# Mixture-of-experts routing on one Trainium2 core: gate products of every second block of nodes on VectorE instead of TensorE

## The reference

```python
# xf: LayerNorm(x), 12500 x 256; 8 experts; the two best of each node are used
logits = xf @ gate_w + gate_b                      # 256 -> 8
probs = softmax(logits)
top2_vals, top2_idx = top_k(probs, 2)
cw = zeros((N, 8)).at[arange(N)[:, None], top2_idx].add(top2_vals)
# for each expert e
out += cw[:, e, None] * (gelu(xf @ W1[e] + b1[e]) @ W2[e] + b2[e])
# result: x + out
```

## Time and profile before

| | |
|---|---|
| median of 3 runs | 3413.88 us (3394.66 to 3414.95) |
| the profiled execution, whole | 3405.85 us |
| its span | 3403.8 us |
| granted TensorE clock, mean over the span | 0.912 of full speed |
| last stage, from the barrier | about 2376 to 3404 us |
| 105 expert slots, 210 adds to `out` on POOL | 332.5 us busy, 1583 ns each |

### The profile page before, as it was taken

One profiled execution on the slowest core, in us unless ns is written; L12 is line 12 of the kernel. 1 busy time (PEld: TensorE's weight loads), 2 busy tenths in 40 slices (PEclk: granted clock), 3 DMA queues, 4 the chain that ended last, 5 costly groups with the idle time before them and its releaser, 6 DMA issues.

```text
span 3403.8 us, 42546 instructions
## 1 busy us (share of the span) xinstructions
PE 2728.9 (80%) x11623; PEld 2100.2 (62%) x11623; DVE 2024.4 (59%) x5319; ACT 1570.9 (46%) x3411; POOL 2264.1 (67%) x2216
## 2 busy tenths in 40 slices
PE   6817767788888888888888878765279999899997
PEld 5706555566665665656665656543158778778886
DVE  7715556766666766766776666677635646544221
ACT  3405543445455455445455445533145555444442
POOL 0077777777777777777777777772647677666444
PEclk9959988899999999998999999887589999999998
DMA  7797766665665665665665665564756666656553
GB/s 237 245 285 217 201 182 164 166 175 159 171 182 155 173 175 160 170 180 161 172 176 163 166 184 157 153 179 100 272 141 165 145 158 165 144 127 138 101 90 48
DMA packets 403513, 570.77 MB, mean 168 GB/s; under 512 B 73177, under 2 KB 320239, under 8 KB 403098
## 3 DMA queue, kind: packets, MB, share of 16 engines
q0 software_dynamic: 125472, 300.85, 35.2%
q1 hardware_dynamic: 200569, 178.04, 17.9%
q10 hardware_dynamic: 77161, 88.52, 9.7%
HBM read 399.19 MB, written 183.46 MB: 171 GB/s over the span
## 4 chain that ended last, share of the span: by engine, by line
PE 57%; DMA 13%; POOL 9%; ACT 8%; issue 7%; DVE 5%; ACTq 1%; SPq 0%; POOLq 0%; DVEq 0%
PE bank L1196 21%; DMA rows<-table,srcix 10%; PE bank L2077 7%; PE bank L2090 7%; PE bank L1007 6%; POOL rows L1132 5%; PE bank L996 4%; PE bank L969 2%; DMA out<-x_y,x_dest 2%; POOL sorted_d L1619 2%; PE bank L784 2%; PE bank L554 1%; PE bank L555 1%; ACT L1232 1%; PE bank L1178 1%
## 5 line engine op out<-in xcount | busy, mean ns | idle before, releaser
L1132 POOL DMA_INDIRECT rows<-table,srcix x1664 | 1609.6, 967 | 506.9 <-issue 358.9
L1196 PE MATMUL bank<-rows,onehot 128*128 128x272 f32 x3328 | 942.7, 430 | 56.0 <-ACT fout L1246 54.3
L1246 ACT ACTIVATE fout<-bank 128x272 f32<-128x272 f32 x1664 | 639.6, 397 | 558.5 <-PE bank L1196 520.3
L1196 PEld LDWEIGHTS bank<-rows,onehot 128*128 128x128 f32 x3328 | 671.7, 210 | 248.5 <-ACT fout L1246 82.0
L1333 DVE TENSOR_TENSOR rows<-rows,bank 128x1024 f32<-128x1024 f32 x416 | 484.2, 1214 | 210.5 <-ACT rows L1237 210.2
L2162 POOL DMA_INDIRECT out<-x_y,x_dest x210 | 332.5, 1583 | 302.8 <-DMA out<-x_y,x_dest 172.0
L2077 PE MATMUL bank<-x_int,x_w1c 128*128 128x256 f32 x1680 | 394.2, 389 | 18.1 <-issue 10.9
L2090 PE MATMUL bank<-e_w,x_ht 128*128 x1680 | 383.7, 382 | 2.3 <-issue 2.3
L2077 PEld LDWEIGHTS bank<-x_int,x_w1c 128*128 128x128 f32 x1680 | 327.1, 196 | 70.0 <-issue 23.7
L2115 ACT ACTIVATE x_ht<-bank,x_b1c 128x256 f32<-128x256 f32 x420 | 174.2, 470 | 370.4 <-PE bank L2077 370.2
L2090 PEld LDWEIGHTS bank<-e_w,x_ht 128*128 128x128 f32 x1680 | 312.7, 191 | 46.3 <-issue 7.6
(11 more groups left out here) (355 smaller groups left out, 3346.9 us busy)
## 6 DMA issues: line engine op xcount, KB each, us to landing
frag<-fout ACTq DMA_DIRECT2D x104, 544.0 KB
x_in<-sorted_d SPq DMA_DIRECT2D x105, 260.0 KB, 3.4
rows<-table,srcix POOLq DMA_INDIRECT x1664
x_b2c<-in_L_ffn_b SPq DMA_DIRECT2D x105, 128.0 KB, 3.7
frag<-in_x ACTq DMA_DIRECT2D x1, 13416.0 KB
table<-hr SPq DMA_DIRECT2D x24, 544.0 KB, 3.6
xs<-in_x SPq DMA_DIRECT2D x24, 512.0 KB, 6.3
xnt_d<-xt SPq DMA_DIRECT2D x24, 512.0 KB, 5.0
```

Source lines behind the costliest of these rows:

```text
L1132: p.indirect_dma_start(out=B.rows[b][:, j, :], out_offset=None, in_=B.table[:, :], in_offset=bass.IndirectOffsetOnAxis(ap=B.srcix[:, col:c ...
L1196: pe.matmul(B.banks[2 + c % 3][:, 0:ROW], B.onehot[k % 2][:, j, :], B.rows[k % NR][:, j, :], start=True, stop=True).then_inc(S.sum, 1)
L1246: a.activation(B.fout[k % 2][:, j, :], B.banks[2 + c % 3][:, 0:ROW], ACT.Copy).then_inc(S.ev, 1)
```

## The change

In rounds 2 to 11 the gate products of the second super no longer go through PE. DVE multiplies each tile's normalized rows (128x256 of `e_hn`) with one expert's gate weights, spread over all partitions in the new `e_gw_all`, and the instruction (`scalar_tensor_tensor` with `accum_out`) also sums the products over the row into one number of `e_lgd`: 8 experts times 4 tiles, 32 instructions a round. `e_gw_all` is laid out [P, D, EXPERTS], so one expert's weights lie 8 words apart. The products themselves go to the scratch tile `e_gw_x`. Each instruction waits for the one before it. `gates` puts them down in 8 groups of 4, three steps apart (`GATES_GAP`), from step `GATES_AT` after the statistics on. Each group waits for its tile's `e_hn`.

PE's turns, gate matmuls and small turns, and ACT's copies, are made for `by_tensor(r)` alone: both supers in rounds 0 and 1, the first super from round 2 on. The bias addition becomes two, one from `e_lgd` and one from PE's bank. `e_hnt` shrinks to one super and `e_lgt` goes (its rows go over the used columns of the turned ones); rounds 0 and 1 use the expert buffers `x_ht`. `e_gw_all` is loaded by one DMA of SP, 1 MB over all partitions, behind the expert weights in round 0.

```diff
+GATES_AT, GATES_GAP = NORM + 4 - MOMENTS - MOMENT_STEPS, 3
+def by_tensor(r):
+    return ROUNDS[r] if r < FIRST_ROUNDS else ROUNDS[r][:1]
 ...
# Bufs
-        self.e_hn, self.e_hnt, self.e_st = several("e_hn", NH, [P, W, SENT]), A("e_hnt", [P, KD, W * P], F32), several("e_st", 2, [P, W, 16])
-        self.lgt = A("e_lgt", [EXPERTS, W * P], F32)
+        self.e_hn, self.e_hnt, self.e_st = several("e_hn", NH, [P, W, SENT]), A("e_hnt", [P, KD, ST * P], F32), several("e_st", 2, [P, W, 16])
+        self.gw_all, self.gw_x = A("e_gw_all", [P, D, EXPERTS], F32), A("e_gw_x", [P, D], F32)
+        self.lgd = A("e_lgd", [P, ST, EXPERTS], F32)
 ...
# route_sync, round 0, behind the loads of W1 and W2
+            sp.dma_start(B.gw_all[:, :, :].rearrange("p d e -> p (d e)"),
+                         B.a["L0_ffn_gate_w"].rearrange("d e -> (d e)").partition_broadcast(P)).then_inc(S.e_wd, 16)
 ...
# route_tensor (route_scalar's copies likewise)
-        for q, k in enumerate(ROUNDS[r]):
+        for q, k in enumerate(mine):          # mine = by_tensor(r)
 ...
-        for i in range(n):
+        for i in range(sum(SUPERS[k][1] for k in mine)):
 ...
# route_vector
+    def gates(r):
+        v.wait_ge(S.e_wd, 16)
+        for k in ROUNDS[r][1:]:
+            s, m = SUPERS[k]
+            for i in range(m):
+                for half in range(2):
+                    v.wait_ge(S.e_hn, s + i + 1)
+                    for e in range(half * EXPERTS // 2, (half + 1) * EXPERTS // 2):
+                        v.wait_ge(vec.sem, vec.n)
+                        vec(v.scalar_tensor_tensor(out=B.gw_x[:, :], in0=B.e_hn[r % NH][:, s - R_FIRST[r] + i, 0:D], scalar=1.0,
+                                                   in1=B.gw_all[:, :, e], op0=ALU.mult, op1=ALU.mult, accum_out=B.lgd[:, i, e:e + 1]))
+                    yield from idle(GATES_GAP)
 ...
+            if len(by_tensor(r)) < len(ROUNDS[r]):
+                own = sum(SUPERS[k][1] for k in ROUNDS[r][1:])
+                yield from idle(GATES_AT)
+                yield from gates(r)
+                waits -= GATES_AT + 2 * own * GATES_GAP
 ...
-        v.tensor_tensor(L, bk[3][:, GATES * EXPERTS:(GATES + n) * EXPERTS].rearrange("p (t e) -> p t e", t=n), over_tiles(B.gb[:, :]), ALU.add).then_inc(S.e_got, 1)
+        if of_pe < n:
+            v.wait_ge(vec.sem, vec.n)
+            vec(v.tensor_tensor(B.lg[:, of_pe:n, :], B.lgd[:, 0:n - of_pe, :], bias(n - of_pe), ALU.add))
+        v.tensor_tensor(B.lg[:, 0:of_pe, :], bk[3][:, GATES * EXPERTS:(GATES + of_pe) * EXPERTS].rearrange("p (t e) -> p t e", t=of_pe),
+                        bias(of_pe), ALU.add).then_inc(S.e_got, 1)
```

More of the change, by code:

```diff
@@ L158, in __init__ @@
             "mg_alpha_spread", "mg_alpha_copied", "mg_run_done", "mg_run_turned", "mg_part_ready", "mg_summed"))
+        self.e_wd = new("e_gate_spread_in")
         self.e_w, self.e_x, self.e_x1 = new("e_gate_in"), several("e_x_in", NF), several("e_x1_out", NF)
@@ L1560, with supers_to, turned @@
 GATES = 2 * P // EXPERTS
+GATES_AT, GATES_GAP = NORM + 4 - MOMENTS - MOMENT_STEPS, 3
 def placed(n):
     return BOTH + LAG + 1 + n + 6
+def by_tensor(r):
+    return ROUNDS[r] if r < FIRST_ROUNDS else ROUNDS[r][:1]
+def supers_to(r):
+    return sum(len(by_tensor(q)) for q in range(r))
 def turns_to(r):
-    return 3 * sum(len(q) for q in ROUNDS[:r])
+    return 3 * supers_to(r)
 def gates_to(r):
-    return sum(len(q) + 1 for q in ROUNDS[:r])
+    return supers_to(r) + r
+def turned(B, r, kk):
+    return B.ht[kk][:, :, :].rearrange("p k n -> p (k n)") if r < FIRST_ROUNDS else B.e_hnt[:, kk, :]
 def at_once(r):
@@ L1690, in steps @@
     def steps(r):
-        n = R_TILES[r]
+        n, mine = R_TILES[r], by_tensor(r)
         yield from idle(TURN)
-        for q, k in enumerate(ROUNDS[r]):
+        for q, k in enumerate(mine):
             s, m = SUPERS[k]
@@ L1702, in steps @@
             yield from idle(TURN_GAP)
-        yield from idle(GATE - TURN - TURN_GAP * len(ROUNDS[r]))
+        yield from idle(GATE - TURN - TURN_GAP * len(mine))
         pe.wait_ge(S.e_w, 32)
-        pe.wait_ge(S.e_t, turns_to(r) + 2 * len(ROUNDS[r]))
-        for i, k in enumerate(ROUNDS[r]):
+        pe.wait_ge(S.e_t, turns_to(r) + 2 * len(mine))
+        for i, k in enumerate(mine):
             s, m = SUPERS[k]
@@ L1709, in steps @@
             for kk in range(KD):
-                t = pe.matmul(bk[i][0:EXPERTS, 0:m * P], B.gw[:, kk, :], B.e_hnt[:, kk, o * P:(o + m) * P], start=(kk == 0), stop=(kk == KD - 1))
+                t = pe.matmul(bk[i][0:EXPERTS, 0:m * P], B.gw[:, kk, :], turned(B, r, kk)[:, o * P:(o + m) * P], start=(kk == 0), stop=(kk == KD - 1))
             t.then_inc(S.e_gate, 1)
@@ L1716, in steps @@
         pe.wait_ge(S.e_carry, r)
-        for i in range(n):
-            t = pe.transpose(bk[3][:, (GATES + i) * EXPERTS:(GATES + i + 1) * EXPERTS], B.lgt[:, i * P:(i + 1) * P],
+        for i in range(sum(SUPERS[k][1] for k in mine)):
+            t = pe.transpose(bk[3][:, (GATES + i) * EXPERTS:(GATES + i + 1) * EXPERTS], turned(B, r, 0)[0:EXPERTS, i * P:(i + 1) * P],
                              B.ident[0:EXPERTS, 0:EXPERTS])
@@ L1736, in steps @@
     def steps(r):
-        x, hn, st = B.e_x[r % NF], B.e_hn[r % NH], B.e_st[r % 2]
+        x, hn, st, theirs = B.e_x[r % NF], B.e_hn[r % NH], B.e_st[r % 2], by_tensor(r)
         yield from idle(NORM)
@@ L1758, in steps @@
         a.wait_ge(S.e_gate, gates_to(r))
-        for i, k in enumerate(ROUNDS[r]):
+        for i, k in enumerate(theirs):
             s, m = SUPERS[k]
@@ L1762, in steps @@
             for kk in range(KD):
-                a.wait_ge(S.e_tp, 2 * (2 * r + i) + kk + 1)
-                a.activation(B.e_hnt[:, kk, o * P:(o + m) * P], bk_columns(B, kk, m), ACT.Copy).then_inc(S.e_t, 1)
+                a.wait_ge(S.e_tp, 2 * (supers_to(r) + i) + kk + 1)
+                a.activation(turned(B, r, kk)[:, o * P:(o + m) * P], bk_columns(B, kk, m), ACT.Copy).then_inc(S.e_t, 1)
             yield from idle(TURN_GAP)
-        yield from idle(GATE + 1 - TURN - TURN_GAP * len(ROUNDS[r]))
-        for i, k in enumerate(ROUNDS[r]):
+        yield from idle(GATE + 1 - TURN - TURN_GAP * len(theirs))
+        for i, k in enumerate(theirs):
             s, m = SUPERS[k]
@@ L1770, in steps @@
             a.wait_ge(S.e_gate, gates_to(r) + i + 1)
-            a.activation(B.lgt[:, o * P:(o + m) * P], B.banks[i][0:EXPERTS, 0:m * P], ACT.Copy).then_inc(S.e_t, 1)
+            a.activation(turned(B, r, 0)[0:EXPERTS, o * P:(o + m) * P], B.banks[i][0:EXPERTS, 0:m * P], ACT.Copy).then_inc(S.e_t, 1)
         yield from idle(FRONT - GATE - 1)
@@ L1846, in steps @@
         v.wait_ge(S.e_w, 32)
-        v.tensor_tensor(L, bk[3][:, GATES * EXPERTS:(GATES + n) * EXPERTS].rearrange("p (t e) -> p t e", t=n), over_tiles(B.gb[:, :]), ALU.add).then_inc(S.e_got, 1)
+        of_pe = sum(SUPERS[k][1] for k in by_tensor(r))
+        bias = lambda m: B.gb[:, :].unsqueeze(1).to_broadcast([P, m, EXPERTS])
+        if of_pe < n:
[3 more added lines that the diff above has]
+                        bias(of_pe), ALU.add).then_inc(S.e_got, 1)
         yield
         v.wait_ge(S.e_got, r + 1)
+        v.wait_ge(vec.sem, vec.n)
         vec(v.tensor_reduce(s1[:, 0:n, 0], L, AX, ALU.max))
```

## The result

| | before | changed |
|---|---|---|
| median of 8 runs | 3412.13 us (3394.66 to 3414.95) | 3431.84 us (3426.83 to 3440.28) |
| ratio to before | | 1.0066, 95% interval 1.0052 to 1.0080 |
| profiled execution, whole | 3405.85 us | 3440.28 us |
| last stage begins (POOL's first memset) | 2375.8 us | 2380.3 us |

The changed kernel is 19.7 us (0.66%) slower. The two profiled executions stand 34 us apart because that of before is 6 us under its median and that of the changed kernel is the slowest of its eight. Their spans, 3403.8 and 3439.0 us, stand 35.2 apart. 4.5 us of that were already there when the last stage began, in code that is the same in both, so the stage itself shows 30.7. What follows adds up these 30.7 us of one pair of executions, not the 19.7 us between the medians.

The account below looks back on a forecast made before the run. POOL's own chain was taken to bound the last stage. +17 us at the start and +30 over eight rounds made 47, less about 8 at the end: net +39 on 3405.85, so 3445 us, range 3400 to 3480.

Parts of the forecast that it names:

- rival 1: Gate stride is free, DVE's round hidden; POOL's stretch, 15 us, and a few us at tile 4 remain: 3420; chance 0.27.
- The bound: Last stage, from tile 3 on: POOL's chain of issues and landings sets the pace; time taken from PE does not shorten it.
- What DVE gets: Rounds 2 to 11: 32 strided products a round, 0.66 us plus 0.08 for the sum; 0.77 each, 24.6 a round.
- The length of a round: Eight full rounds: DVE's list and waits take 64.8 us or more against 62.6; +3.7 a round, 30 us together.
- a sign that the prediction named against itself: The forecast is wrong if DVE keeps 10 us or more of idle time a round.
- The second price: POOL issues beginning within two-input gates are stretched, 0.25 us each, 2 to 3 us a round; not added.
- the sign against the queue: POOL's lag above 15 us through rounds 5 to 11 while the total grows: then the stretch is the price.
- The start: Rounds 2 and 3: gates delay the first tiles, +7 and +10 us, +17 in all.
- The end: After the last product: POOL is less behind, so the last 21.9 us shrink by about 8.
- Rival 2: PE was the bound, so its 31 us saving comes through and DVE hides the gates: 3375; chance 0.06.
- Rival 3: Sum needs a second pass, 35 us a round, or POOL and DVE hold each other whole instructions: 3535; chance 0.07.

Follow-up runs that it names:

- the first set: Four variants of the changed kernel (control, no gates, one-input gates, PE not relieved), timed against the kernel before, which took 3411.6 us: ratios 1.0063, 0.9986, 1.0028, 1.0065.
- the kernel nearest to before in the second set: Kernel before, its product by the node's weight made by two one-SBUF-input instructions: 3895.1 us, ratio 1.0034.
- the second set: Gates from round 4, contiguous weights, doubled gates, and the kernel before with one-input product, against the kernel before at 3882.8 us: 0.9926, 0.9935, 1.0428, 1.0034.
- the third set: Changed kernel, no gates, gates from round 4, and that with contiguous weights, against the kernel before at 3848.9 us: 0.9917, 0.9956, 0.9927, 0.9960.

## Why the prediction was right or wrong, point by point

The time, 3431.8 against a forecast of 3445 in a range of 3400 to 3480, and its sign came out; the way to it did so only in part. The nearness is partly luck. The forecast was +39 us, put on the one profiled execution of 3405.85, which is 6 us under the median; between the medians +19.7 were measured, half of it. In the profiled executions the stage grew by 30.7 us: 7.5 up to round 2's logits, 1.8 in round 3, 18.3 in the eight rounds, -0.5 in the next, nothing in the tail up to the last product, and 3.6 behind it. I had 17, 30 and -8. What happened is close to the mechanism of rival 1 (3420, +14), though not for its reason, since the stride was not free: the gates fit beside the rest, and POOL's stretch and some us at tile 4 are left.

- **The bound (POOL's chain, PE's relief worth nothing).** Right in the first set, and shown there: 2.8 us of 31 came through without gates, nothing beside them. In the other two sets it did not hold.
- **What DVE gets.** Right. 0.625 us for the product, where I had 0.66 from the statistics' strides (contiguous 0.425, so the stride does cost, 0.20 where I had 0.23), 0.083 for the read-out, where I had 0.08. The total is 0.68 a gate instead of 0.77, because the read-out overlaps its product's end and I had counted it and 0.03 us more in full.
- **The length of a round.** This step failed: "Together +3.7 a round, 30 us over eight", by DVE's list. It came to +2.3, and not by DVE's list. DVE is busy 53.5 us a round, its short pauses are 3.7, and its waits for ACT and PE were 11.0 us at the head of the gates, 9.2 for the counts, 2.6 for the exponent and 0.9 for PE's product over all eight rounds, 3.0 a round. So it needs 60.2, under POOL's 62.6. I had 64.8: about 1.1 too much for the work itself, 1.1 for the wait at the head of the gates and 2.2 for the other waits. The margin is small, and 4.8 us a round of DVE's idle time of 11.5 stand in front of POOL itself, in 12 waits of `x_dest` for a free product buffer. That idle time of over 10 us a round is a sign that the prediction named against itself.

- **The second price.** I held it to be as large as the first ("2 to 3 us a round") and did not add the two, which was right: it is the one that was paid. The issues grew by 15 us, near 1.9 a round over eight; what of it reached the time is between 10 and 15 us, by the run with one-input gates. This is what the last sentence of the prediction named as the sign against the queue: a lag above 15 us all through, with a total that grows.
- **The start.** +7 in round 2 and +10 in round 3. Round 2's logits came 7.5 us later (2514.7 - 2380.3 = 134.4 from the stage's beginning, against 2502.7 - 2375.8 = 126.9), round 3 took 56.7 instead of 54.9, so +2 and not +10. Tile 4's product was finished 15.8 us later, measured from the stage's beginning, near the 17 that I had for DVE. At POOL it is 11.3, since POOL's lag of 5.4 there took up the rest: I named that lag and then charged the whole 17. The idle time of 6.78 us at tile 4 is where I had put it; that its moment fits so well (2571.8, forecast 2573) is luck, since 4.5 us of it arose before the stage.
- **The end.** -8 was wrong: POOL's lag at the last tile is 20.8, not nearer to 10, and from the last product to the end it took 25.5 us instead of 21.9. It followed from the failed step, since DVE did not set the pace.
- **Rival 2 (PE was the bound)** fell in the first set. In the other two its direction came out, with 0.9917 for the changed kernel, but without gates only half of the saving came through. Its condition was a lag of POOL below about 3 us in most rounds. In the kernel nearest to before in the second set that held for 77 of 102 tiles, and in the third set without gates for 71, with gates for 9.
- **Rival 3** fell: 320 gates lay between 0.61 and 0.71 us, 6 of them above 0.64, so POOL held none up for longer than 0.1 us; POOL's side waits.

## What to carry to other kernels

Moving work from a busy engine to one with idle time pays only if the busy engine is the one that is waited for last: 98% busy PE had 31 us taken away and gave back 3, since POOL stood behind it, 17 to 34 us late with finished work in hand. What the new work reads matters as much as how long it takes: the same 0.62 us in the same places cost 27 us with two SBUF inputs and 12 with one, because POOL was issuing DMAs beside it. A verdict of less than 1% changed its sign from one set of runs to another, so it should come with the time that the kernel before took beside it. And before a wait is called a wait for nothing, compare the end of the wait with the ends of the other engines' instructions: the record of the releaser may only be missing.

## What the runs showed that I had not expected

- The hold is nearly one-sided and short. An issue of POOL that begins inside a gate is longer by 0.14 us (sends) or 0.16 (adds), where 0.22 and 0.20 us of the gate were left to run; DVE's instruction is hardly longer for it (0.71 us at most against a mean of 0.625). Over 504 issues it came to 16 us, 12 of them in issues that met a gate.
- The same program took 3411.6, 3882.8 and 3848.9 us in the three sets, 14% apart, and the change reversed its sign: 1.0066, and 0.9917 in the last. In the second set PE was idle for 82 us over nine rounds instead of 26, nearly always until an instruction of ACT had ended. What made the sets differ was not found.
- In the third set the 160 us of gate work on DVE went with a higher granted clock of PE (0.96 against 0.93) and 40 us less for nine rounds. This is unexplained, too.
